# Who copies the first two key projections of a batch out of PSUM: ScalarE or VectorE

## The chip, the cores and the metric

One NeuronCore of a Trainium2 chip runs the whole program. The metric is the device time of one execution in microseconds (us).

## What is computed

The input has 32 batches of 256 tokens with 128 features. Each batch passes a layer norm, then an attention block with 16 heads of 64, and a feed-forward block beside it; both are added to the input.

```python
xn = _layernorm(x, axis=-1)
# attention on rmsnorm(xn) * norm_w:
q = x @ Wq;  k, v = jnp.split(x @ Wkv, 2, axis=-1)       # each 256 x 1024 per batch
q = _head_rmsnorm(q, q_gamma);  k = _head_rmsnorm(k, k_gamma)
sim = jnp.tanh(jnp.einsum('bhid,bhjd->bhij', q, k) / 50) * 50 * 64 ** -0.5
out = jnp.einsum('bhij,bhjd->bhid', jax.nn.softmax(sim), v)   # then @ Wo
# feed-forward: gelu(xn @ W1.T + low-rank part + b1) @ W2.T + low-rank part + b2
x = x + attention + feed_forward
```

## The kernel before

The engines run in a software pipeline over the batches. A period works on batch n in attention ("attn"), on n+1 in "front" (the second half of its projections, squares, norms, transposes of the heads), on n+2 in "turn" (its first projections), loads n+3 and finishes n-1. A period has eight steps, one for each pair of heads; the five lists TENSOR_STEPS, SCALAR_STEPS, VECTOR_STEPS, POOL_STEPS and the sync engine's loop say what each engine issues in each step, and in which order. The lists are in-order programs: an instruction that waits holds up everything behind it on its engine.

The names that matter here:

- **scores** (PE, L511) are the 12 matmuls of one pair into ps_scores; **tanh** (ACT, L597, tile clamped) reads them, **exp** (ACT, L604, tile probs) follows; **values** (PE, L537 to L539) multiplies probabilities with v two steps later into ps_o; **divide** (DVE, L772 and L776) takes ps_o out into o_sb.
- **q, k, v** with a number 0 to 3 are the projections of one batch: 128 tokens by 512 columns each, three matmuls L431, L432, L433 into one of three PSUM banks, ps_aux. Banks are used in turn, in the order of the tuples of three in TENSOR_STEPS, and `wait_bank` makes PE wait until the user three places back has been read.
- A **q** is squared by ACT (L623) and scaled by DVE (L799). A **v** is copied in bf16 by ACT (L633) and its remainder made by DVE (L804). A **k** is copied to qk by ACT (L628) and squared by POOL (L967); the sums of the squares are DVE's (L714).
- **normalise** (DVE, L755) writes a pair to ps_n, **half** (ACT, L612) makes its fp16 part and **halves** (DVE, L763) the remainder; two DMA transposes on the sync engine's queue (L396) then turn them for the scores three steps later.

By the order of the banks, k 0, k 1, v 2 stand in banks 0, 1, 2, and behind them v 3, q 2, q 3, and then k 2, k 3 and oT 0 of the next period. So in step 6 and the two steps behind it:

- v 3 waits until k 0 has been copied, q 2 until k 1 has;
- q 3 waits for DVE's part of v 2, k 2 for DVE's part of v 3;
- k 3 waits until q 2 has been scaled by DVE, oT 0 until q 3 has.

PE's step 6, for reference:

```python
    [("scores",), ("values",), ("k", 0, 2), ("k", 1, 2), ("y", 2), ("v", 2, 1), ("v", 3, 1)],
```

Of the kernel before, what the change touches and what calls it, by code (L numbers as in the profile page):

```python
# [32 lines left out]
PAIRS = HEADS // 2  # L33
# [43 lines left out]
    [("half", 3), ("tanh",), ("oT", 3, -1), ("exp",), ("half", 4), ("hid", 0, 0), ("hid", 1, 0)],  # L77
    [("tanh",), ("q", 0, 2), ("exp",)],
    [("half", 3), ("tanh",), ("q", 1, 2), ("exp",), ("v", 0, 1), ("v", 1, 1)],
    [("half", 3), ("tanh",), ("exp",), ("k", 0, 2), ("k", 1, 2), ("v", 2, 1)],  # L80
    [("half", 3), ("tanh",), ("v", 3, 1), ("exp",), ("q", 2, 2)],
]
VECTOR_STEPS = [
# [5 lines left out]
    [("divide",), ("newton", 5), ("newton", 6), ("newton", 7), ("newton", 8), ("normalise",), ("norm_stats",),  # L89
     ("q", 0, 2)],  # L90
    [("halves", 3), ("divide",), ("normalise",), ("q", 1, 2), ("sum", 0, 2), ("v", 0, 1)],
    [("halves", 3), ("v", 1, 1), ("divide",), ("normalise",), ("sum", 1, 2), ("v", 2, 1)],
    [("halves", 3), ("divide",), ("normalise",), ("v", 3, 1), ("sum", 2, 2), ("sum", 3, 2)],
]
POOL_STEPS = [
# [50 lines left out]
def block_kernel(nc, tokens, norm_w, wq, wkv, wo, q_gamma, k_gamma, w1, b1, w2, b2, scale, out):  # L146
# [6 lines left out]
    with ExitStack() as ctx:  # L153
# [50 lines left out]
        qk = sb("qk", [P, 2, TT, QK])  # L204
# [69 lines left out]
        qk_normed = sem("qk_normed")  # L274
# [7 lines left out]
        aux_filled = {k: sem(f"{k}_filled") for k in PER_BATCH}  # L282
        xT_split = sem("xT_split")
        xnT_copied = sem("xnT_copied")
        k_copied = sem("k_copied")
# [19 lines left out]
        def wait(eng, s, value):  # L305

            if isinstance(value, int) and value <= 0:
                return
            eng.wait_ge(s, value)
# [281 lines left out]
        @block.scalar  # L591
        def _(act):
            def tanh(st, pair):
                b, _, _ = st.batch(0)
                wait(act, scores_done, 2 * PAIRS * b + 2 * pair + 2)
                wait(act, probs_done, PAIRS * b + pair)
                nc.scalar.activation(clamped[:].rearrange("p j n -> p (j n)"),  # L597
                                     ps_scores[:].rearrange("p j n -> p (j n)"), ACT.Tanh).then_inc(clamp_done, 1)

            def exp(st, pair):  # L600
                b, _, _ = st.batch(0)
                wait(act, clamp_done, PAIRS * b + pair + 1)
                wait(act, attended, PAIRS * b + pair + 1 - RING)
                nc.scalar.activation(probs[:, pair % RING].rearrange("p j n -> p (j n)"),  # L604
                                     clamped[:].rearrange("p j n -> p (j n)"), ACT.Exp, bias=LIFT,
                                     scale=SOFTCLAMP * DH ** -0.5).then_inc(probs_done, 1)

            def half(st, ahead, pair):
                b, _, _ = st.batch(ahead)
                act.wait_ge(qk_normed, PAIRS * b + pair + 1)  # L610
                wait(act, heads_turned[pair % 4], 32 * ((PAIRS * b + pair) // 4))
                nc.scalar.copy(halves16[:, pair % 4, 0].rearrange("p a n -> p (a n)"), ps_n[:]).then_inc(half_hi_made, 1)  # L612

            def aux(st, kind, k, ahead):
                b, par, _ = st.batch(ahead)
                bank = bank_of(kind, k)
                act.wait_ge(aux_filled[kind], PER_BATCH[kind] * b + k + 1)
                if kind == "xT":
                    nc.scalar.copy(xhT_hi[:, par], bank[:, 0:seq])
                    nc.scalar.copy(xnT[:, b % 3], bank[:, seq:2 * seq]).then_inc(xnT_copied, 1)  # L620
                elif kind == "q":
                    wait(act, norm2_made, 8 * (b - 1) + 4 * (k // 2) + k % 2 + 1)
                    nc.scalar.activation(sq_q[:, k], bank, ACT.Square).then_inc(q_squared, 1)  # L623
                elif kind == "k":
                    if k == 0:
                        wait(act, qk_normed, PAIRS * (b - 1))
                    t, c = k // 2, 2 + k % 2
                    nc.scalar.copy(qk[:, par, t, c * 512:(c + 1) * 512], bank).then_inc(k_copied, 1)  # L628
                elif kind == "v":
                    if k == 0:  # L630
                        wait(act, attended, PAIRS * (b - 1))
                    t, c = k // 2, k % 2
                    nc.scalar.copy(v_hi[:, par, t, 8 * c:8 * c + 8, 0:DH],  # L633
                                   bank.rearrange("p (h d) -> p h d", d=DH)).then_inc(v_hi_made, 1)
                elif kind == "oT":
                    nc.scalar.copy(oT[:, 2 * k:2 * k + 2], bank.rearrange("p (j t) -> p j t", j=2))\
                        .then_inc(oT_copied, 1)
                elif kind == "hid":
                    for j in range(2):
                        c = 2 * k + j  # L640
                        nc.scalar.activation(hid[:, par, c], bank[:, j * seq:(j + 1) * seq], ACT.Gelu,  # L641
                                             bias=b1_col[:, c:c + 1]).then_inc(gelu_done, 1)

            def run(st):
                for s in range(PAIRS):
                    for what, *k in SCALAR_STEPS[s]:
                        if what == "tanh":
                            if "attn" in st.stages:
                                tanh(st, s)
                        elif what == "exp":  # L650
                            if "attn" in st.stages:
                                exp(st, s)
                        elif what == "half":
                            normed = ahead_of(st, s, *k)
                            if normed:
                                half(st, *normed)
                        elif STAGE[k[1]] in st.stages and (st.number > -2 or what != "xT"):
                            aux(st, what, *k)

            def weights_hi(c):  # L660
                part = slice(c * HEADS * DH, (c + 1) * HEADS * DH)
                act.wait_ge(w_scaled, c + 1)
                nc.scalar.copy(w_hi[:, part], w_raw[:, part]).then_inc(w_hi_made, 1)

            weights_hi(0)
            weights_hi(1)
            aux(Step(-1, 0, ()), *XT_TASK[1:])
            act.wait_ge(gammas_spread, 1)
            for j in range(2):
                nc.scalar.copy(g_bc[:, j * 512:(j + 1) * 512], ps_scores[:, j]).then_inc(gammas_copied, 1)  # L670
            weights_hi(2)
            act.wait_ge(ffn_turned, 1)
            nc.scalar.copy(b1_col[:], ps_o[:, 0:HC]).then_inc(ffn_copied, 1)
            nc.scalar.copy(w1T[:].rearrange("p a b -> p (a b)"), ps_scores[:, 0]).then_inc(ffn_copied, 1)
            nc.scalar.copy(w2T[:].rearrange("p a b -> p (a b)"), ps_scores[:, 1]).then_inc(ffn_copied, 1)
            act.wait_ge(ffn_copied, 3)
            run_all(act, run)
# [3 lines left out]
        def _(dve):  # L681
            v = nc.vector
# [106 lines left out]
            def aux(st, kind, k, ahead):  # L789
                b, par, _ = st.batch(ahead)  # L790
                bank = bank_of(kind, k)
                if kind == "xT":
                    xT_lo(st, bank)
                elif kind == "q":
                    dve.wait_ge(q_squared, 4 * b + k + 1)
                    if k == 0:
                        wait(dve, qk_normed, PAIRS * (b - 1))
                    t, c = k // 2, k % 2
                    v.tensor_tensor(qk[:, par, t, c * 512:(c + 1) * 512], bank, g_bc[:, c * 512:(c + 1) * 512],  # L799
                                    ALU.mult).then_inc(q_scaled, 1)  # L800
                elif kind == "v":
                    dve.wait_ge(v_hi_made, 4 * b + k + 1)
                    t, c = k // 2, k % 2
                    v.tensor_tensor(v_lo[:, par, t, 8 * c:8 * c + 8], bank.rearrange("p (h d) -> p h d", d=DH),  # L804
                                    v_hi[:, par, t, 8 * c:8 * c + 8, 0:DH], ALU.subtract).then_inc(v_split, 1)
                elif kind == "low":
                    dve.wait_ge(aux_filled["low"], 2 * b + k + 1)
                    if k == 1:
                        wait(dve, y_filled, b - 1)
                    o, base = (w1_eff[:], w1T) if k == 0 else (w2_eff[:, par], w2T)  # L810
                    v.scalar_tensor_tensor(o, bank.rearrange("p (c n) -> p c n", c=HC), scale_col[:, 0:1], base[:],
                                           ALU.mult, ALU.add)\
                        .then_inc(weff_made, 1)
# [220 lines left out]
```

## Time and profile before

| | |
|---|---|
| time, median of 3 runs | 1099.09 us (1098.5 to 1099.18) |
| the profiled execution | 1098.77 us, of which the span of the profile is 1096.6 us |
| PE (matmul) busy | 1048.1 us, 96% of the span |
| ACT busy | 1033.9 us, 94% |
| DVE busy | 928.6 us, 85% |
| POOL busy | 852.4 us, 78% |

PE is TensorE's matmuls, PEld its weight loads, ACT is ScalarE, DVE is VectorE, POOL is GpSimd, SPq the sync engine's DMA queue. A busy share says how full an engine is over the whole span; which engine sets the pace of a stage is read from the waits, the chain of work that ended last and the rows in order of time. In rows in order of time the first number is the start, the second the duration of the row (of all its instructions, for x2 and more), and square brackets give idle time just before it and who ended it. An instruction can start some 0.09 us before the end of the one ahead of it on its engine, because the ends overlap.

### The profile page before, as it was taken

The page shows a single profiled execution, that of the slowest core. Times are in us where ns is not written, and L with a number is a line of the kernel's source. Part 1 is how long each engine was busy: PE and PEld are TensorE (multiplying, and loading weights), DVE is VectorE, ACT ScalarE, POOL GpSimd, SP SyncE. Part 2 cuts the span into 40 slices and gives each one's busy share as a digit, 9 for nine tenths or more (in the row PEclk, how much of TensorE's full clock was granted, in tenths as well). Part 3 has the DMA queues.
Part 4 walks back from the last instruction along what each step waited for, and adds up shares of the span by engine and source line. Part 5 has one row for each costly group of instructions (what it writes and reads, how often), then busy time and mean ns, then how long its engine had stood idle before and what let it go on. Part 6 is the DMA issues. An engine that isn't in the chain of part 4 may idle for free.

```text
span 1096.6 us, 33887 instructions
## 1 busy us (share of the span) xinstructions
PE 1048.1 (96%) x12889; PEld 842.7 (77%) x12889; DVE 928.6 (85%) x2185; ACT 1033.9 (94%) x1545; POOL 852.4 (78%) x784
## 2 busy tenths in 40 slices
PE   5789999999999999999999999999999999999987
PEld 4467787777787777787777788777787777787776
DVE  6988889888889888889888889888889888889872
ACT  4699999999999999999999999999999999999996
POOL 7677878887878887878887878887878887878763
PEclk9899999999999999999999999999999999999999
DMA  3344444344454334444334444434444334344341
GB/s 114 65 72 81 74 85 80 71 78 84 74 84 80 74 77 82 75 85 79 75 75 84 75 84 80 72 77 84 76 83 79 78 71 84 76 82 80 65 92 31
DMA packets 310487, 85.41 MB, mean 78 GB/s; under 512 B 282020, under 2 KB 309816, under 8 KB 310328
## 3 DMA queue, kind: packets, MB, share of 16 engines
q1 hardware_dynamic: 310328, 83.25, 39.8%
q8 instruction: 104, 1.70, 0.7%
q14 instruction: 55, 0.45, 0.2%
HBM read 11.09 MB, written 4.19 MB: 14 GB/s over the span
## 4 chain that ended last, share of the span: by engine, by line
PE 42%; ACT 38%; issue 11%; SPq 2%; DVE 2%; POOL 2%; DMA 2%; ACTq 0%; POOLq 0%
ACT clamped L597 11%; PE ps_scores L511 10%; ACT probs L604 9%; PE ps_aux L486 5%; PE ps_aux L431 4%; PE ps_y L559 4%; ACT L641 4%; ACT halves L612 4%; ACT L604 4%; PE ps_o L537 3%; PE ps_aux L433 3%; PE ps_aux L432 3%; ACT hid L641 3%; PE ps_o L539 2%; PE ps_o L538 2%
## 5 line engine op out<-in xcount | busy, mean ns | idle before, releaser
L973 POOL TENSOR_TENSOR probs_lo<-probs 128x1024 f16<-128x1024 f32 x256 | 485.1, 1895 | 208.1 <-ACT probs L604 208.1
L597 ACT ACTIVATE clamped<-ps_scores 128x1024 f32<-128x1024 f32 x256 | 265.9, 1039 | 24.9 <-PE ps_scores L511 20.9
L604 ACT ACTIVATE probs<-clamped 128x1024 f32<-128x1024 f32 x256 | 273.0, 1066 | 2.6
L763 DVE TENSOR_TENSOR halves<-ps_n,halves 128x512 f16<-128x512 f32 x256 | 174.9, 683 | 65.9 <-ACT halves L612 65.8
L537 PEld LDWEIGHTS ps_o<-v_hi,probs 128*128 128x128 bf16 x2048 | 183.9, 98 | 60.9 <-issue 58.4
L511 PE MATMUL ps_scores<-heads_T 64*128 64x256 f16 x3072 | 212.2, 271 | 11.8 <-ACT clamped L597 6.1
L537 PE MATMUL ps_o<-v_hi,probs 128*128 128x65 bf16 x2048 | 213.8, 195 | 5.5 <-POOL probs_lo L973 1.4
L538 PE MATMUL ps_o<-v_lo,probs 128*128 128x64 bf16 x2048 | 211.7, 193 | 0.0
L539 PE MATMUL ps_o<-v_hi,probs_lo 128*128 128x65 bf16 x2048 | 211.3, 194 | 0.0
L431 PE MATMUL ps_aux<-w_hi,xhT_hi 128*128 128x512 f32 x384 | 178.9, 466 | 19.3 <-ACT qk L628 6.8
L538 PEld LDWEIGHTS ps_o<-v_lo,probs 128*128 128x128 bf16 x2048 | 187.3, 98 | 0.0
L539 PEld LDWEIGHTS ps_o<-v_hi,probs_lo 128*128 128x128 f16 x2048 | 187.2, 97 | 0.0
L511 PEld LDWEIGHTS ps_scores<-heads_T 64*128 64x128 f16 x3072 | 131.6, 94 | 65.6 <-issue 33.6
L755 DVE TENSOR_TENSOR ps_n<-qk,ps_o 128x512 f32<-128x512 f32 x256 | 175.8, 687 | 1.3
L612 ACT CAST halves<-ps_n 128x512 f16<-128x512 f32 x256 | 153.5, 599 | 3.8 <-DVE ps_n L755 3.4
L432 PE MATMUL ps_aux<-w_lo,xhT_hi 128*128 128x512 f32 x384 | 153.0, 398 | 0.0
L433 PE MATMUL ps_aux<-w_hi,xhT_lo 128*128 128x512 f32 x384 | 152.9, 398 | 0.0
L559 PEld LDWEIGHTS ps_y<-wo_sb,oT 128*128 128x128 f32 x1024 | 143.1, 191 | 10.5
L559 PE MATMUL ps_y<-wo_sb,oT 128*128 128x128 f32 x1024 | 150.3, 275 | 0.0
L967 POOL TENSOR_TENSOR sq_k<-qk 128x512 f32<-128x512 f32 x128 | 130.7, 1042 | 3.3 <-ACT qk L628 3.3
L431 PEld LDWEIGHTS ps_aux<-w_hi,xhT_hi 128*128 128x128 f32 x384 | 73.2, 191 | 69.8 <-DVE v_lo L804 25.3
L776 DVE TENSOR_TENSOR o_sb<-ps_o,rden 128x256 f32<-128x256 f32 x256 | 108.6, 424 | 8.8
(83 smaller groups left out, 1910.8 us busy)
## 6 DMA issues: line engine op xcount, KB each, us to landing
heads_T<-halves SPq DMA_TRANSPOSE x512, 2.5
x_in<-in_L_attn_tokens_dram SPq DMA_DIRECT2D x32, 128.0 KB, 2.4
x_res<-in_L_attn_tokens_dram SPq DMA_DIRECT2D x32, 128.0 KB, 2.3
out_dram<-y_sb SPq DMA_DIRECT2D x32, 128.0 KB, 2.0
sel_raw<-xn SPq DMA_DIRECT2D x192, 4.0 KB
qk<-in_L_attn_Wkv_dram SPq DMA_DIRECT2D x2, 512.0 KB, 5.6
qk<-in_L_attn_Wq_dram SPq DMA_DIRECT2D x1, 512.0 KB, 3.6
qk<-in_L_ffn_W_dram SPq DMA_DIRECT2D x2, 256.0 KB
```

Of the source, the lines that this page charges most:

```text
L431: pe.matmul(o, hi_l, hi_r, start=True, stop=False)
L432: pe.matmul(o, hi_l, lo_r, start=False, stop=False)
L433: return pe.matmul(o, lo_l, hi_r, start=False, stop=last)
L511: ins = pe.matmul(ps_scores[:, odd, t * seq:(t + 1) * seq], heads_T[rows, left, pair, t, k], heads_T[rows, right, pair, :, q], start=(i == ...
L537: pe.matmul(full, hi[:, col], v_hi[:, par, u, h], start=(u == 0), stop=False)
L538: pe.matmul(full[:, 0:DH], hi[:, col], v_lo[:, par, u, h], start=False, stop=False)
L539: ins = pe.matmul(full, probs_lo[:, buf, j, col], v_hi[:, par, u, h], start=False, stop=(u == TT - 1))
L559: ins = pe.matmul(o, oT[:, pair, tok], wo_sb[:, pair], start=False, stop=(i == n - 1))
L597: nc.scalar.activation(clamped[:].rearrange("p j n -> p (j n)"), ps_scores[:].rearrange("p j n -> p (j n)"), ACT.Tanh).then_inc(clamp_done, 1)
L604: nc.scalar.activation(probs[:, pair % RING].rearrange("p j n -> p (j n)"), clamped[:].rearrange("p j n -> p (j n)"), ACT.Exp, bias=LIFT, ...
L612: nc.scalar.copy(halves16[:, pair % 4, 0].rearrange("p a n -> p (a n)"), ps_n[:]).then_inc(half_hi_made, 1)
L973: g.tensor_tensor(probs_lo[:, buf].rearrange("p j n -> p (j n)"), probs[:, buf].rearrange("p j n -> p (j n)"), probs[:, buf].rearrange("p ...
```

## The change

ScalarE's step 6 loses the copies of k 0 and k 1. VectorE's step 6 gets them: k 0 between divide and normalise, k 1 between normalise and the sum of squares. The copies of k 2 and k 3, in step 0, stay with ScalarE. The semaphore k_copied is still counted in order, so each side waits for the other's earlier copies.

```diff
@@ SCALAR_STEPS, step 6
-    [("half", 3), ("tanh",), ("exp",), ("k", 0, 2), ("k", 1, 2), ("v", 2, 1)],
+    [("half", 3), ("tanh",), ("exp",), ("v", 2, 1)],
@@ VECTOR_STEPS, step 6
-    [("halves", 3), ("v", 1, 1), ("divide",), ("normalise",), ("sum", 1, 2), ("v", 2, 1)],
+    [("halves", 3), ("v", 1, 1), ("divide",), ("k", 0, 2), ("normalise",), ("k", 1, 2), ("sum", 1, 2), ("v", 2, 1)],
@@ scalar, aux
                 elif kind == "k":
-                    if k == 0:
-                        wait(act, qk_normed, PAIRS * (b - 1))
+                    wait(act, qk_normed, PAIRS * (b - 1))
+                    wait(act, k_copied, 4 * b + k)
@@ vector, aux
+                elif kind == "k":
+                    dve.wait_ge(aux_filled["k"], 4 * b + k + 1)
+                    if k == 0:
+                        wait(dve, qk_normed, PAIRS * (b - 1))
+                        wait(dve, k_copied, 4 * b)
+                    t, c = k // 2, 2 + k % 2
+                    v.tensor_copy(qk[:, par, t, c * 512:(c + 1) * 512], bank).then_inc(k_copied, 1)
```

VectorE's instructions in step 6 and the start of step 7 of a period, before. The rows begin with halves of step 6 and end with the scaling of q 2 and q 3 in step 0 of the next period (names in brackets are the semaphores waited for):

```order
L763 TENSOR_TENSOR halves16<-ps_n,halves16 128x512 [waits half_hi_made]
L804 TENSOR_TENSOR v_lo<-ps_aux,v_hi 128x512 [waits v_hi_made]
L772 RECIPROCAL rden<-ps_o 128x4 [waits attended]
L776 TENSOR_TENSOR o_sb<-ps_o,rden 128x2x128 [waits rden_made]
L755 TENSOR_TENSOR ps_n<-qk,ps_o 128x512 [waits half_lo_made]
L714 TENSOR_REDUCE norm2<-sq_q 128x8 [waits q_squared]
L804 TENSOR_TENSOR v_lo<-ps_aux,v_hi 128x512 [waits v_hi_made]
L763 TENSOR_TENSOR halves16<-ps_n,halves16 128x512 [waits half_hi_made]
L772 RECIPROCAL rden<-ps_o 128x4 [waits attended]
...
L799 TENSOR_TENSOR qk<-ps_aux,g_bc 128x512 [waits q_squared] x2
```

The same stretch on VectorE after the change (the two COPY rows are L807; what was L804 is now L811):

```order
L763 TENSOR_TENSOR halves16<-ps_n,halves16 128x512 [waits half_hi_made]
L811 TENSOR_TENSOR v_lo<-ps_aux,v_hi 128x512 [waits v_hi_made]
L772 RECIPROCAL rden<-ps_o 128x4 [waits attended]
L776 TENSOR_TENSOR o_sb<-ps_o,rden 128x2x128 [waits rden_made]
L807 COPY qk<-ps_aux 128x512 [waits k_copied,qk_normed,k_filled]
L755 TENSOR_TENSOR ps_n<-qk,ps_o 128x512 [waits half_lo_made]
L807 COPY qk<-ps_aux 128x512 [waits k_filled]
L714 TENSOR_REDUCE norm2<-sq_q 128x8 [waits q_squared]
L811 TENSOR_TENSOR v_lo<-ps_aux,v_hi 128x512 [waits v_hi_made]
L763 TENSOR_TENSOR halves16<-ps_n,halves16 128x512 [waits half_hi_made]
L772 RECIPROCAL rden<-ps_o 128x4 [waits attended]
...
L799 TENSOR_TENSOR qk<-ps_aux,g_bc 128x512 [waits q_squared] x2
```

Two copies stand ahead of everything from the sum of squares on, and one ahead of normalise; the order of the rest is the same.

ScalarE's step 6 before, from tanh to the half of step 7:

```order
L597 ACTIVATE clamped<-ps_scores 128x1024 [waits probs_done,scores_done]
L604 ACTIVATE probs<-clamped 128x1024 [waits attended,clamp_done]
L628 COPY qk<-ps_aux 128x512 [waits qk_normed,k_filled]
L628 COPY qk<-ps_aux 128x512 [waits k_filled]
L633 CAST v_hi<-ps_aux 128x8x64 [waits v_filled]
L612 CAST halves16<-ps_n 128x512 [waits heads_turned2,qk_normed]
```

And after:

```order
L597 ACTIVATE clamped<-ps_scores 128x1024 [waits probs_done,scores_done]
L604 ACTIVATE probs<-clamped 128x1024 [waits attended,clamp_done]
L633 CAST v_hi<-ps_aux 128x8x64 [waits v_filled]
L612 CAST halves16<-ps_n 128x512 [waits heads_turned2,qk_normed]
```

The bf16 copy of v 2 and the half of step 7 stand right behind exp. PE's, POOL's and the sync engine's programs are the same as before.

## Rows read from the trace of the kernel before

**Rows 1.** Busy time in nine stretches of 100 us: their sum and mean.

```profile
sum 900.00, PE 884.79 PEld 713.51 DVE 784.97 ACT 875.84 POOL 720.65; mean PE 98.31 PEld 79.28 DVE 87.22 ACT 97.32 POOL 80.07
```

**Rows 2.** Waits, whole span: total us, times, longest us.

```profile
PEld ps_aux L431 <- ACT qk L628: 20.3, 31, 1.1
...
PE ps_aux L431 <- ACT qk L628: 6.8, 31, 0.7
```

**Rows 3.** The chain that ended last, 500 to 570 us: start, us, what.

```profile
528.60 0.58 ACT qk L628
...
529.22 0.50 PE ps_aux L431
...
545.54 0.82 ACT clamped L597
```

**Rows 4.** ACT in order of time, steps 6 and 7 of one period.

```profile
528.60 1.06 ACT L628 COPY qk<-ps_aux 128x512 f32<-128x512 f32 x2
529.54 0.60 ACT L633 CAST v_hi<-ps_aux 128x512 bf16<-128x512 f32 x1
530.02 0.61 ACT L612 CAST halves<-ps_n 128x512 f16<-128x512 f32 x1
531.02 1.03 ACT L597 ACTIVATE clamped<-ps_scores 128x1024 f32<-128x1024 f32 x1 [0.39 <-PE ps_scores L511]
```

**Rows 5.** PE in order of time: v 2's last, v 3's first, k 3's first matmul.

```profile
528.62 0.40 PE L433 MATMUL ps_aux<-w_hi,xhT_lo 128*128 128x512 f32 x1
529.22 0.50 PE L431 MATMUL ps_aux<-w_hi,xhT_hi 128*128 128x512 f32 x1 [0.20 <-ACT qk L628]
...
536.13 0.46 PE L431 MATMUL ps_aux<-w_hi,xhT_hi 128*128 128x512 f32 x1
```

**Rows 6.** DVE in order of time, from halves of step 6 to q 2.

```profile
526.71 0.69 DVE L763 TENSOR_TENSOR halves<-ps_n,halves 128x512 f16<-128x512 f32 x1 [0.19 <-ACT halves L612]
...
528.12 0.42 DVE L776 TENSOR_TENSOR o_sb<-ps_o,rden 128x256 f32<-128x256 f32 x1
528.46 0.69 DVE L755 TENSOR_TENSOR ps_n<-qk,ps_o 128x512 f32<-128x512 f32 x1
529.05 0.68 DVE L714 TENSOR_REDUCE norm<-sq_q 128x8 f32<-128x512 f32 x1
530.18 0.69 DVE L804 TENSOR_TENSOR v_lo<-ps_aux,v_hi 128x512 bf16<-128x512 f32 x1 [0.45 <-ACT v_hi L633]
530.78 0.68 DVE L763 TENSOR_TENSOR halves<-ps_n,halves 128x512 f16<-128x512 f32 x1
531.82 0.18 DVE L772 RECIPROCAL rden<-ps_o 128x4 f32<-128x4 f32 x1 [0.35 <-PE ps_o L539]
...
535.36 1.27 DVE L799 TENSOR_TENSOR qk<-ps_aux,g_bc 128x512 f32<-128x512 f32 x2
```

**Rows 7.** PE's weight loads in order of time: the first of k 3.

```profile
536.09 0.19 PEld L431 LDWEIGHTS ps_aux<-w_hi,xhT_hi 128*128 128x128 f32 x1 [0.23 <-DVE qk L799]
```
**Rows 8.** DVE by form, whole span: busy us, mean ns of one, idle before.

```profile
L799 DVE TENSOR_TENSOR qk<-ps_aux,g_bc 128x512 f32<-128x512 f32 x128 | 83.9, 676 | 2.5 <-ACT sq_q L623 2.3 <-issue 0.2
...
L811 DVE SCALAR_TENSOR_TENSOR w_eff<-ps_aux,scale_col,w1T 128x512 f32<-128x512 f32 x32 | 23.7, 742 | 0.0
...
L737 DVE TENSOR_TENSOR ps_o<-newton_r,ps_o 128x64 f32<-128x64 f32 x96 | 21.7, 226 | 2.2
...
L727 DVE TENSOR_SCALAR newton_r<-ps_o 128x64 int32<-128x64 int32 x32 | 7.2, 224 | 1.1
```

**Rows 9.** DVE in order of time, before the first period.

```profile
13.13 0.78 DVE L818 TENSOR_SCALAR qk<-qk,nw_col 128x1024 f32<-128x1024 f32 x1
...
21.62 0.69 DVE L714 TENSOR_REDUCE norm<-sq_k 128x8 f32<-128x512 f32 x1 [0.91 <-POOL sq_k L967]
...
38.24 0.69 DVE L804 TENSOR_TENSOR v_lo<-ps_aux,v_hi 128x512 bf16<-128x512 f32 x1 [0.48 <-ACT v_hi L633]
```

**Rows 10.** Sync engine's queue in order of time, step 0 of the next period.

```profile
538.55 2.52 SPq L396 DMA_TRANSPOSE heads_T<-halves  x2
```

## The prediction

> **What bounds the kernel now.** I began with the busy time by stretches. Between 100 and 1000 us the mean is PE 98.3, ACT 97.3, DVE 87.2 of 100 us [rows 1]. Two engines are full and the third has room, so the change looks like relief for a full one. Shares can't say which of the two holds the end in which step, so I read the chain of work next. Two hand-overs repeat in it in every period [rows 3]. At 529.22 the chain goes from ACT's copy of k 0 (528.60 + 0.58 = 529.18) to PE's first matmul of v 3; from there PE holds it through steps 7, 0, 1 and 2 until tanh of step 3 at 545.54, and from there ACT holds it to step 6 again. So **ACT sets the pace from step 3 to the middle of step 6, PE from there to step 3**. The waits over the whole span say the same: a matmul of the L431 kind waits for ACT's k copy 31 times, once per period, 20.3 us by the weight loads and 6.8 us by the matmuls [rows 2].
>
> Then I read one period in order of time. PE ends v 2 and sits idle 0.20 us until k 0 is out of its bank [rows 5]. Matmuls of that kind follow each other with a spacing of some 0.24 us, so v 3 could have begun at 528.62 + 0.24 = 528.86, and the wait is worth 0.36 us at most. ACT, behind its two copies, gets to v 2 and half, and then waits 0.39 us for PE's scores of step 7 [rows 4]: time given back to ACT here is waited away.
>
> **The change on ScalarE.** Two copies go, 1.06 us together, some 0.94 us of queue (528.60 to 529.54, [rows 4]). What is gained there is not 30 x 0.94: tanh of step 7 is held by PE. The only thing that PE waits for is k 0's bank. v 2's bf16 copy now comes as soon as PE has filled the bank: 528.62 + 0.40 = 529.02, so it ends at about 529.65 instead of 530.14.
>
> **The change on VectorE.** What does one copy cost there? No row shows a single-source 512-column DVE instruction out of PSUM. The nearest are the 512-column ones with one PSUM operand: 676 ns for the scaling of q, 742 ns for the scalar_tensor_tensor [rows 8]. In the queue they cost less, since ends overlap: normalise at 528.46, the next at 529.05, 0.595 us apart [rows 6]. From below: a single-source instruction from SBUF to SBUF took 0.78 us for 1024 columns [rows 9], twice as fast per column, which for 512 would be some 0.78 - 0.27 = 0.51 us long, 0.42 in the queue. Does that rate hold out of PSUM? The 64-column rows say no: a column costs (676 - 226) / 448 = 1.0 ns in tensor_tensor, so double rate would make a single-source 64-column instruction some 32 ns shorter than a tensor_tensor; the one that reads PSUM (L727) takes 224 ns against 226 [rows 8]. I take 0.595 us in the queue and 0.68 us from start to end; the bounds are 0.42 and 0.66 (742 ns less the same overlap).
>
> The Trainium skill (VectorE: DVE Perf Modes, Why PSUM operands drop a tier) says that a PSUM operand caps fp32 at the single rate. The 224 ns row agrees. Its cycle table gives 120 + 512 cycles, an estimate of 658 ns for the copy; with it each number below would be about 0.02 us smaller. At the double rate the sum would have the other sign, which is the second rival.
>
> **k 0's hand-over.** DVE starts k 0 where normalise started, at 528.46; its bank was full long before. It ends at 529.14 against 529.18 on ACT. PE gains 0.04 us of the 0.36. The reason is that DVE comes to k 0 only behind halves, v 1 and divide, and halves had waited for ACT's half (idle 0.19 before 526.71, [rows 6]); ACT was the pace-setter up to there, so that start doesn't move.
>
> **DVE's debt.** Two copies push everything behind them by 2 x 0.595 = 1.19 us. Two gaps take some of it. Between the sum at 529.05 and v 2's remainder at 530.18 there is 1.13 us where 0.595 is needed: 0.53 spare (it was the wait for ACT's v 2, which now comes early enough). Between halves at 530.78 and the reciprocal at 531.82, 1.04 where 0.60 is needed: 0.44 spare; this was the wait for PE's values, and they end no later than before. Together 0.97. The debt left is 1.19 - 0.97 = **0.22 us**. From 531.82 to 535.36 no row shows idle time, so it is carried whole to the scaling of q 2: start 535.57 instead of 535.36, end 536.25 instead of 535.36 + 0.68 = 536.04.
>
> **Who waits for it.** PE's k 3 uses q 2's bank. Before, its weights were loaded at 536.09, just 0.05 us behind the end of q 2's scaling, after 0.23 us of waiting [rows 7], and its matmul came at 536.13, with no time lost to speak of [rows 5]. DVE was exactly on time, with nothing to spare. Now the load comes at 536.30 and the matmul at 536.30 to 536.34: PE is late by 0.17 to 0.21 us, in the stretch that PE sets. Behind k 3, q 3's scaling holds oT 0 by the same amount, nothing more is lost there, and PE carries the delay to tanh of step 3 and so into the period. The 0.04 us gained at v 3 drowns in the wait for q 2.
>
> The other waiters have slack. k 1 is out at about 530.3 and q 2 is multiplied behind the values at 531.6. Remainders of v 2 and v 3 end 0.65 and 0.2 us later, still ahead of q 3 and k 2. Halves of step 7 is 0.65 us later (531.43); its transposes are for scores three steps on, and the sync queue is itself behind: the next pair's transposes are issued at 538.55 [rows 10], three us after their halves. Normalise of step 6 is 0.6 us later, at 529.05 to 529.74; half of step 7 started at 530.02. POOL's squares start behind probs_lo.
>
> **Sum.** Batches whose k 0 and k 1 are projected beside attention: 30 of 32 (two are in the fill). 30 x 0.2 = 6.0 us. In the fill DVE is the longest: for the first batch the copies stand behind the weight split instead of beside it, and 0.9 us of idle before the sums [rows 9] takes most of it, about 0.25 left; for the second the debt is 1.19 less the 0.48 + 0.09 before v 2's remainder, 0.6, of which I count 0.5. Total 6.0 + 0.75 = 6.75 us on the profiled execution's 1098.77: 1105.5. The median of the runs is 0.3 us above that execution, so **1105.8 us**, 0.6% slower. With the bounds of the copy's cost: at 0.66 the debt is 0.35, 10.5 us and 1 in the fill, 1110.6; a debt of zero needs 0.485.
>
> **Rivals.**
> - *The debt is lost in slack.* If rests of a few hundredths between DVE's instructions or an earlier start of its chain take most of the 0.22, only the fill is left: 1099.09 + 0.75 = 1099.8, no change. For it: 0.22 is a small difference of large numbers. Against: no idle shown from 531.82 to 535.36. Chance 0.12.
> - *The copy is fast* (faster than before). A single-source DVE copy out of PSUM at double rate: 0.42 in the queue. Debt 0.84, all absorbed by 0.97; k 0 is out at 528.46 + 0.51 = 528.97, PE starts v 3 at 529.01, 0.21 earlier; 30 x 0.21 = 6.3, 1092.8 us. It decides below 0.485 us in the queue. For it the 0.78 row, against it the 224 ns row. Chance 0.06.
> - *ScalarE is what counts.* If its 0.94 us came off each period: 30 x 0.94 = 28, 1071 us. Against: its 0.39 us wait in step 7 and the PE-held chain. 0.02.
> - *More than the debt gets through:* the 0.65 us lateness of halves in step 7 reaches the scores through the sync queue, 30 x 0.65 = 19.5, 1119 us. Against: three steps between. 0.05.
>
> **How the numbers follow.** The forecast has 0.75. Its own spread (debt 0.1 to 0.35, fill 0.3 to 1.2) is 1102.4 to 1110.6; the range 1101.5 to 1110 holds it and the edge of the first rival. Within 0.2% (2.2 us) is about what a measurement of this kernel can tell from no change: faster 0.08, same 0.13, slower 0.79.
>
> **What the changed profile would show.** DVE's k copies at about 0.68 us each; k 0 ending 0.04 us sooner in the period than ACT's did; the reciprocal of step 7 no longer waiting for PE; PE's L431 matmuls waiting for DVE's scaling of q, some 0.2 us, 30 times, in step 0; ACT idle about 0.5 to 1 us more in steps 6 and 7 of each period; one batch to the next about 0.2 us longer. I am wrong if the copy takes clearly less than 0.6 us, if DVE shows idle time between step 6's halves and q 2's scaling, or if PE waits at another place.

## The result and the profile after

| | before | changed |
|---|---|---|
| median | 1098.8 us (4 runs, 1098.25 to 1099.18) | 1105.86 us (4 runs, 1105.18 to 1106.12) |
| ratio | | 1.0064, 95% interval 1.0046 to 1.0081 |
| profiled execution, its span | 1098.77, 1096.6 us | 1105.18, 1103.1 us |

The changed kernel is slower by 7 us, 0.64%, at the same granted clock (0.995 in both profiles). Its page begins so (busy time and instructions of each engine, then the chain of work that ended last, by engine):

```profile
PE 1056.0 (96%) x12889; PEld 844.7 (77%) x12889; DVE 961.5 (87%) x2249; ACT 1012.1 (92%) x1481; POOL 851.6 (77%) x784
...
PE 34%; ACT 34%; DVE 22%; issue 9%; DMA 0%; ACTq 0%; SPq 0%; POOL 0%
```

ACT has lost 22 us of work, DVE has gained 33 us. The chain tells more than the shares: DVE is only 87% busy, but it holds 22% of the chain now, where it held 2% before:

```profile
PE 42%; ACT 38%; issue 11%; SPq 2%; DVE 2%; POOL 2%; DMA 2%; ACTq 0%; POOLq 0%
```

The mean by stretches, beside [rows 1], shows the same with PE as full as ever:

```profile
sum 900.00, PE 885.30 PEld 709.66 DVE 808.20 ACT 853.14 POOL 717.78; mean PE 98.37 PEld 78.85 DVE 89.80 ACT 94.79 POOL 79.75
```

The chain in order of time (start, us, what) has three hand-overs per period now, where [rows 3] had two. ACT gives to DVE at halves of step 6, DVE holds it for 9.6 us, and PE gets it at k 3, which waits for the scaling of q 2:

```profile
529.88 0.64 ACT halves L612
530.54 0.69 DVE halves L763
...
539.48 0.61 DVE qk L799
540.13 0.50 PE ps_aux L431
...
549.58 0.81 ACT clamped L597
```

DVE in that stretch, to be laid beside [rows 6]:

```profile
530.54 0.69 DVE L763 TENSOR_TENSOR halves<-ps_n,halves 128x512 f16<-128x512 f32 x1 [0.18 <-ACT halves L612]
...
531.95 0.42 DVE L776 TENSOR_TENSOR o_sb<-ps_o,rden 128x256 f32<-128x256 f32 x1
532.29 0.68 DVE L807 COPY qk<-ps_aux 128x512 f32<-128x512 f32 x1
532.89 0.69 DVE L755 TENSOR_TENSOR ps_n<-qk,ps_o 128x512 f32<-128x512 f32 x1
533.48 0.68 DVE L807 COPY qk<-ps_aux 128x512 f32<-128x512 f32 x1
534.09 0.67 DVE L714 TENSOR_REDUCE norm<-sq_q 128x8 f32<-128x512 f32 x1
534.68 0.68 DVE L811 TENSOR_TENSOR v_lo<-ps_aux,v_hi 128x512 bf16<-128x512 f32 x1
535.28 0.68 DVE L763 TENSOR_TENSOR halves<-ps_n,halves 128x512 f16<-128x512 f32 x1
535.88 0.17 DVE L772 RECIPROCAL rden<-ps_o 128x4 f32<-128x4 f32 x1
...
539.40 1.28 DVE L799 TENSOR_TENSOR qk<-ps_aux,g_bc 128x512 f32<-128x512 f32 x2
```

Both gaps of [rows 6] are gone, in front of v 2's remainder and in front of the reciprocal. Measured from the start of halves in step 6, q 2 is scaled at 539.40 - 530.54 = 8.86 us, before at 535.36 - 526.71 = 8.65. PE, matmuls and then the weight load of k 3, beside [rows 5, 7]:

```profile
533.03 0.50 PE L431 MATMUL ps_aux<-w_hi,xhT_hi 128*128 128x512 f32 x1 [0.18 <-DVE qk L807]
...
540.13 0.50 PE L431 MATMUL ps_aux<-w_hi,xhT_hi 128*128 128x512 f32 x1
```
```profile
540.13 0.19 PEld L431 LDWEIGHTS ps_aux<-w_hi,xhT_hi 128*128 128x128 f32 x1 [0.49 <-DVE qk L799]
```

v 3 starts 2.49 us behind halves (before 2.51), k 3 9.59 us (before 9.42): 0.02 us gained, 0.17 lost. k 3's own first matmul costs 0.04 more as well: the next one follows after 0.34 us, before after 0.30. Its weights are loaded only as it starts (both rows at 540.13), before 0.04 us ahead. The matmul's row shows no idle time, since the end of the matmul ahead of it is modelled; the weight load's row shows the wait. Medians over 25 periods say the same: k 3's first matmul is 0.19 us later behind halves than before, its second 0.22, and PE's instructions stay 0.21 to 0.22 later to the end of the period. So the whole loss of a period arises at k 3.

ACT, beside [rows 4], has waits of 0.35 and 0.63 us where there was one of 0.39, and tanh of step 7 starts 4.28 us behind halves, before 4.31. The 0.94 us of queue that the two copies left free is waited away:

```profile
532.88 0.59 ACT L633 CAST v_hi<-ps_aux 128x512 bf16<-128x512 f32 x1 [0.35 <-PE ps_aux L433]
533.61 0.58 ACT L612 CAST halves<-ps_n 128x512 f16<-128x512 f32 x1
534.82 1.03 ACT L597 ACTIVATE clamped<-ps_scores 128x1024 f32<-128x1024 f32 x1 [0.63 <-PE ps_scores L511]
```

The whole span's waits (total us, times, longest): behind the scaling of q the weight loads waited 16.2 us before and 24.2 now. The 20.3 us behind ACT's k copy [rows 2] are now 20.0 us behind DVE's, so that wait has changed its releaser and not its size:

```profile
PEld ps_aux L431 <- DVE qk L799: 24.2, 35, 3.6
PEld ps_aux L431 <- DVE qk L807: 20.0, 31, 1.5
```

A copy took what the prediction took for it (by form: busy us, mean ns):

```profile
L807 DVE COPY qk<-ps_aux 128x512 f32<-128x512 f32 x64 | 43.6, 682 | 0.5 <-PE ps_aux L433 0.5
```

**The account of the two spans.** I date a period by the start of v 0's remainder on DVE. From one batch to the next it is 32.86 us before and 33.07 us after. In the profile of before three of 29 periods were longer, by 0.34, 0.23 and 0.41 us; after, none. The first period with all stages begins at 65.47 us before and at 66.73 us after; behind the last start both need the same 45.45 us. So the spans differ by 1.26 (fill) + 30 x 0.205 (6.15) - 0.98 (the three long periods of before) = 6.4 us, against 1103.1 - 1096.6 = 6.5.

The 1.26 us of the fill are the net of two things. Ahead of PE's only long wait for a transpose in the fill, PE is 1.73 us late (L492 at 50.82, before at 49.09). Then the transposes come, and PE waits 0.84 us for them, before 1.94:

```profile
52.05 0.86 PE L511 MATMUL ps_scores<-heads_T 64*128 64x256 f16 x12 [0.84 <-DMA heads_T<-halves]
```
```profile
51.41 0.83 PE L511 MATMUL ps_scores<-heads_T 64*128 64x256 f16 x12 [1.94 <-DMA heads_T<-halves]
```

### The profile page after: what moved, and what is told of

The parts are those of the page before. It is cut to its first block, busy times and chain, and to the rows that moved or that the text cites. A ratio compares the mean times of both kernels' runs of the same rounds, so it can differ in the third digit from the quotient of the medians.

```text
span 1103.1 us, 33952 instructions
## 1 busy us (share of the span) xinstructions
PE 1056.0 (96%) x12889; PEld 844.7 (77%) x12889; DVE 961.5 (87%) x2249; ACT 1012.1 (92%) x1481; POOL 851.6 (77%) x784
## 4 chain that ended last, share of the span: by engine, by line
PE 34%; ACT 34%; DVE 22%; issue 9%; DMA 0%; ACTq 0%; SPq 0%; POOL 0%
ACT probs L604 9%; ACT clamped L597 8%; PE ps_scores L511 8%; PE ps_aux L486 5%; DVE halves L763 5%; DVE v_lo L811 4%; DVE norm L714 4%; ACT L641 4%; ACT halves L612 4%; ACT L604 4%; PE ps_y L559 3%; DVE qk L807 3%; PE ps_aux L431 3%; ACT hid L641 3%; DVE ps_n L755 3%
## 5 line engine op out<-in xcount | busy, mean ns | idle before, releaser
L763 DVE TENSOR_TENSOR halves<-ps_n,halves 128x512 f16<-128x512 f32 x256 | 174.9, 683 | 65.5 <-ACT halves L612 65.4
```

The costliest lines, as they stand in the source:

```text
L763: v.tensor_tensor(halves16[:, pair % 4, 1].rearrange("p a n -> p (a n)"), ps_n[:], halves16[:, pair % 4, 0].rearrange("p a n -> p (a n)"), ...
```

## The experiments

The period is read from each kernel's trace in the same way (one execution each); ratios are to the kernel before on the same chip (medians 1098.64, 1099.56 and 1098.69 us for the three groups of four). "Few waits" means: without the added waits on ScalarE that the order doesn't need.

| kernel | median us | ratio, 95% interval | period us |
|---|---|---|---|
| two blanks on VectorE | 1103.85 | 1.0049, 1.0036 to 1.0063 | 33.05 |
| three blanks | 1122.06 | 1.0213, 1.0199 to 1.0227 | 33.65 |
| k 0 alone on VectorE | 1100.29 | 1.0014, 1.0005 to 1.0023 | 32.88 |
| k 1 alone on VectorE | 1101.96 | 1.0024, 1.0013 to 1.0035 | 32.91 |
| changed, q 2 scaled first | 1101.51 | 1.0021, 1.0013 to 1.0030 | 32.93 |
| changed, k 0 ahead of divide | 1105.59 | 1.0062, 1.0050 to 1.0075 | 33.06 |
| k 0 on VectorE ahead of divide, k 1 on ScalarE | 1088.12 | 0.9898, 0.9886 to 0.9911 | 32.47 |
| before, k 0 ahead of exp | 1085.87 | 0.9880, 0.9865 to 0.9894 | 32.39 |
| k 0 alone, few waits | 1098.12 | 0.9993, 0.9984 to 1.0002 | 32.83 |
| k 0 ahead of divide, few waits | 1087.22 | 0.9894, 0.9882 to 0.9907 | 32.47 |
| changed, few waits | 1104.75 | 1.0058, 1.0046 to 1.0070 | 33.07 |
| fill only | 1099.42 | 1.0004, 0.9995 to 1.0012 | 32.85 |

**Two and three blank instructions.** The debt on VectorE without any move of a copy, against the kernel before (the lines that allocate blank and its semaphore are left out; three blanks have a `("blank", 2)` behind the second, and 3 in place of 2 in the wait):

```diff
-    [("halves", 3), ("v", 1, 1), ("divide",), ("normalise",), ("sum", 1, 2), ("v", 2, 1)],
+    [("halves", 3), ("v", 1, 1), ("divide",), ("blank", 0), ("normalise",), ("blank", 1), ("sum", 1, 2), ("v", 2, 1)],
+                        elif what == "blank":
+                            if "attn" in st.stages and "turn" in st.stages:
+                                wait(dve, blank_made, 2 * st.batch(0)[0])
+                                v.tensor_reduce(blank[:, k[0]], g_bc[:, 0:512].rearrange("p (h d) -> p h d", d=DH),
+                                                AX_X, ALU.add).then_inc(blank_made, 1)
```

> The kernel before, with two more VectorE instructions per period and nothing else: a 512-column reduce that nobody reads stands where the changed kernel has its copies of k 0 and k 1 (behind divide, behind normalise of step 6). ScalarE keeps both copies. Theory (VectorE's debt: 2 x 0.595 less 0.97 of gaps is 0.22 us, which reaches PE at k 3): the loss of the change without its relief and without its cost in the fill, 30 x 0.2 = 6 us, less up to 1 us for three periods that were irregular before: 1104 to 1105 us, k 3's matmul of step 0 about 0.2 us late behind q 2's scaling. Rival (the loss comes from who copies k: a hand-over of semaphores between two engines, PSUM read by VectorE): no change, 1099.

> The same with a third reduce behind the second. The gaps are used up by the second, so the third should be paid whole: debt 3 x 0.595 - 0.97 = 0.81 us, 30 x 0.8 = 24, 1122 us. If the waits merely get longer where there is slack elsewhere, less than 1115.

Two blanks give a period of 33.05 us, 0.02 from the changed kernel's, though ScalarE does all its old work. The third adds 0.60 us per period, a whole instruction's share of the queue. The waits of weight loads and matmuls behind the scaling of q, with two blanks:

```profile
PEld ps_aux L433 <- DVE qk L801: 22.2, 35, 2.1
...
PE ps_aux L433 <- DVE qk L801: 6.3, 6, 1.4
```

and with three:

```profile
PEld ps_aux L433 <- DVE qk L801: 40.1, 35, 2.1
...
PE ps_aux L433 <- DVE qk L801: 24.2, 35, 1.4
```

With two, the wait shows on the weight loads and hardly on the matmuls; with three the matmuls wait too, in every period, at the named place. Who copies k, and across which semaphore, has at most 0.02 us in the period's loss of 0.21. The median with two blanks, 1103.85, is just under my 1104, that with three as expected.

**One copy alone.** k 0 (`("k", 1, 2)` back on ScalarE behind exp) and k 1 (`("k", 0, 2)` back). The edit for k 0, step 6 of ScalarE and then of VectorE, against the kernel before; the waits of the change stay, and VectorE's copy waits for the count `4 * b + k` of k_copied (not shown):

```diff
-    [("half", 3), ("tanh",), ("exp",), ("k", 0, 2), ("k", 1, 2), ("v", 2, 1)],
+    [("half", 3), ("tanh",), ("exp",), ("k", 1, 2), ("v", 2, 1)],
-    [("halves", 3), ("v", 1, 1), ("divide",), ("normalise",), ("sum", 1, 2), ("v", 2, 1)],
+    [("halves", 3), ("v", 1, 1), ("divide",), ("k", 0, 2), ("normalise",), ("sum", 1, 2), ("v", 2, 1)],
```

> Only k 0 moves to VectorE (same place, behind divide); k 1 stays with ScalarE behind exp. Theory: one copy is 0.595 us, less than the 0.97 of gaps, so no debt; PE gets k 0's bank 0.04 us earlier, 31 x 0.04 = 1.2 us gained, some of it given back in the fill: 1097.5 to 1099.5. Rival (a copy ahead of normalise delays halves and scores, and this is what costs): about half of the loss of the change or more, 1102 to 1105.

> Only k 1 moves to VectorE (behind normalise); k 0 stays with ScalarE behind exp. Theory: no debt, and k 0's hand-over is where it was: 1098.5 to 1099.5. Rival as for k 0 alone, now with the copy behind normalise: if the loss is due to the copy in front of normalise, this one is free and the other isn't; by the debt both are free.

In the period both are nearly free (0.02 and 0.05 us), and the one behind normalise is no cheaper than the one in front of it. k 3's first matmul comes 9.38 and 9.41 us behind halves (medians), before 9.41: no debt reaches it. But both medians missed my ranges on the slow side, and that of k 1, 1101.96, comes near the rival's 1102; only the periods tell the two apart. I had a gain of 0.04 per period for k 0 and nothing for k 1. Laid period on period from halves of step 6, k 0's kernel is 0.02 us ahead of the one before, and k 1's level with it, up to PE's second oT in step 1; from there they are 0.04 and 0.06 us behind. ACT shows why (k 0's kernel: k 1, which waited for the count of DVE's k 0; then k 2 and k 3 of step 0):

```profile
530.78 0.59 ACT L628 COPY qk<-ps_aux 128x512 f32<-128x512 f32 x1 [0.56 <-DVE qk L807]
...
538.36 1.26 ACT L628 COPY qk<-ps_aux 128x512 f32<-128x512 f32 x2
```

From the start of k 2 to the end of k 3 it takes 1.26 us, 1.06 before; the change put two more semaphore waits in front of each. The copies themselves are no longer (0.56 and 0.58 us; before 0.57 and 0.59). k 3 starts later: here k 2 runs from 538.36 to 538.92 and k 3 starts at 539.03; before, k 3 started at 537.32, ahead of the end of k 2 at 537.42.

```profile
539.03 0.58 ACT L628 COPY qk<-ps_aux 128x512 f32<-128x512 f32 x1
```
```profile
537.32 0.59 ACT L628 COPY qk<-ps_aux 128x512 f32<-128x512 f32 x1
```

The count `4 * b + 3` of k_copied for which k 3 waits is the one that k 2's copy gives, so ScalarE waits for its own last instruction and loses the overlap with it (k 3's other added wait, for qk_normed, was not tried apart). k 2 starts 0.97 us behind exp with or without the added waits. tanh of step 1 and the oT behind it slip by what is left.

The profiled execution of k 1's kernel was 4.2 us longer than that of the kernel before; it was the longest of its seven. Its first full period begins 3.8 us later and its periods are 30 x 0.05 us longer, against the 0.98 us of the three long periods before. In the fill PE waited 2.73 us once for a transpose of the heads, at a place where it waited 1.94 before; why that transpose was later there stays open.

**Few waits.** Only those that the order of the two engines needs, in three of the kernels, against the change (where both copies are on VectorE, the condition is k == 2 and the wait is the one for k_copied alone):

```diff
-                    wait(act, qk_normed, PAIRS * (b - 1))
-                    wait(act, k_copied, 4 * b + k)
+                    if k == 1:
+                        wait(act, qk_normed, PAIRS * (b - 1))
+                        wait(act, k_copied, 4 * b + k)
```

> k 0 alone on VectorE, as before, but ScalarE's copies of k 2 and k 3 in step 0 no longer carry the two extra semaphore waits each that the change gave them. In the trace of k 0 alone those two copies took 1.26 us instead of 1.06, tanh of step 1 came 0.14 us later, and from PE's second oT on (step 1) everything was 0.06 us later, which would be the difference between the 0.02 us gained at v 3 and the 0.025 us lost per period. Theory: the waits cost it, so a period of 32.83 to 32.85 us instead of 32.88, 1098 to 1099.3 with the fill. Rival (something else, ScalarE's wait for k_copied in front of k 1 say): 32.88 as before, 1100.3.

> The changed kernel with as few waits in front of ScalarE's k 2 and k 3 as the order of the two engines allows (one). There PE is 0.2 us late at k 3, so that ScalarE's 0.14 us in step 1 should be hidden: 33.06 us per period and 1105 to 1106.5 as before. If the waits were part of the loss: 33.01 or less, 1104.

> k 0 on VectorE ahead of divide, k 1 on ScalarE, without the extra waits in front of k 2 and k 3. Theory: 0.05 us per period less than the 32.47 with them, near the 32.39 of ScalarE's k 0 ahead of exp: 1086 to 1087. Rival: 32.47, 1088.

With k 0 alone, k 2 and k 3 are back at 1.05 us, and the time came out as expected:

```profile
536.32 1.05 ACT L629 COPY qk<-ps_aux 128x512 f32<-128x512 f32 x2
```

and the period at 32.83, 0.03 below before. The changed kernel keeps its 33.07: there PE is late anyway. Its k 2 still waits for k_copied, its k 3 no longer, and the two are back at 1.06 us, so it is the wait in front of k 3 that cost. Its median, 1104.75, is 1 us lower and a little under my range, within the scatter of the two. The third was a miss: 32.47 stayed, so in that kernel something else sets the period (next but one).

**Where the debt reaches PE.** The changed kernel with q 2 scaled one place earlier (VectorE's step 0), and with k 0 copied one place earlier (its step 6), each against the change:

```diff
-    [("halves", 3), ("q", 2, 1), ("q", 3, 1), ("divide",), ("normalise",), ("result",), ("sum", 4, 1)],
+    [("q", 2, 1), ("halves", 3), ("q", 3, 1), ("divide",), ("normalise",), ("result",), ("sum", 4, 1)],
```
```diff
-    [("halves", 3), ("v", 1, 1), ("divide",), ("k", 0, 2), ("normalise",), ("k", 1, 2), ("sum", 1, 2), ("v", 2, 1)],
+    [("halves", 3), ("v", 1, 1), ("k", 0, 2), ("divide",), ("normalise",), ("k", 1, 2), ("sum", 1, 2), ("v", 2, 1)],
```

> The changed kernel, with one exchange on VectorE in step 0: q 2 is scaled ahead of halves instead of behind it, so 0.60 us earlier. Theory (PE pays at k 3, which waits for q 2): k 3 is on time again, q 3 (for oT 0) is still 0.2 us late but its matmuls need it 0.7 us after k 3, so at most 0.05 us per period is left: the fill's 1.3 us and 0 to 1.5 us, 1099 to 1101.5. Rival (the debt reaches PE by normalise or halves and the scores): no better than the changed kernel, 1106, or worse since halves is later still.

> The changed kernel with k 0 copied ahead of divide instead of behind it. PE gets the bank 0.55 us earlier, so v 3 starts about 0.3 us earlier than in the kernel before. Theory: VectorE's chain from step 6 to q 2 has the same length, so this is wasted at k 3: 1105.5 to 1106.5, with PE's wait at q 2 about 0.3 us longer. Rival (k 0's late hand-over is what costs): 0.3 x 31 = 9 us gained, 1097.

The exchange of two neighbours in step 0 takes the period from 33.07 to 32.93, two thirds of the loss, with not an instruction less on DVE. PE's medians behind halves show where the 0.07 left arise. k 3's second matmul is now 0.09 us earlier than in the kernel before; oT 0, which waits for q 3 (first row below), is 0.02 later, and the scores behind it 0.07. From PE's second oT in step 1 on, where the added wait on ACT showed in the lone copies, at most 0.02 more is lost. So nearly all of it is q 3; I had expected 0.05 at most.

Freeing k 0's bank one place earlier, 0.55 us, on the other hand, brings nothing: PE starts v 3 0.34 us sooner than in the changed kernel and waits the longer for q 2, with k 3 at 9.60 us behind halves in both (last two rows; 24.2 and 7.0 us in the changed kernel):

```profile
PEld ps_aux L486 <- DVE qk L799: 11.7, 30, 0.7
```
```profile
PEld ps_aux L431 <- DVE qk L799: 38.3, 35, 3.7
...
PE ps_aux L431 <- DVE qk L799: 22.9, 35, 3.2
```

**The same early bank, without the debt.** k 0 on VectorE ahead of divide, k 1 on ScalarE (step 6 of ScalarE, then of VectorE, against the kernel before; the waits as for k 0 alone):

```diff
-    [("half", 3), ("tanh",), ("exp",), ("k", 0, 2), ("k", 1, 2), ("v", 2, 1)],
+    [("half", 3), ("tanh",), ("exp",), ("k", 1, 2), ("v", 2, 1)],
-    [("halves", 3), ("v", 1, 1), ("divide",), ("normalise",), ("sum", 1, 2), ("v", 2, 1)],
+    [("halves", 3), ("v", 1, 1), ("k", 0, 2), ("divide",), ("normalise",), ("sum", 1, 2), ("v", 2, 1)],
```

And with ScalarE alone, the kernel before with one copy moved:

```diff
-    [("half", 3), ("tanh",), ("exp",), ("k", 0, 2), ("k", 1, 2), ("v", 2, 1)],
+    [("half", 3), ("tanh",), ("k", 0, 2), ("exp",), ("k", 1, 2), ("v", 2, 1)],
```

> k 0 on VectorE ahead of divide, k 1 on ScalarE behind exp. Theory: one copy makes no debt, and PE's wait for k 0's bank (0.36 us at most) is gone, with the steps behind it 0.3 us earlier: 31 x 0.3 = 9 us, 1089 to 1091. It is less if the sync queue's transposes, which made PE wait in three periods of the kernel before, can't follow: then 1093 to 1097.

> The kernel before, with ScalarE's copy of k 0 between tanh and exp of step 6 instead of behind exp; nothing on VectorE. Theory: k 0's bank is free at 528.2 instead of 529.18, v 3 doesn't wait, 31 x 0.35 = 11 us at best; exp of step 6 is 0.5 us later, for which POOL has some room: 1088 to 1091. The same bound by the transposes as in the run before: 1093 to 1097.

Both beat both kernels, 1.0% and 1.2% faster than before, and both are faster than I had expected (1089 and 1088 at best). The first, in the version with few waits, shows why waits no longer matter to it. DVE runs without a gap again:

```profile
523.35 0.68 DVE L808 COPY qk<-ps_aux 128x512 f32<-128x512 f32 x1
...
526.28 0.68 DVE L764 TENSOR_TENSOR halves<-ps_n,halves 128x512 f16<-128x512 f32 x1
526.88 0.17 DVE L773 RECIPROCAL rden<-ps_o 128x4 f32<-128x4 f32 x1
```

The reciprocal follows halves at once, for PE's values are earlier too. One copy (0.6) in 0.97 of gaps leaves 0.38, and 0.39 is what the period lost. PE agrees: its instructions behind v 3 come 0.48 us earlier behind halves than before, up to k 3; there the weight load waits for q 2 (row below), and 0.38 is left. So DVE sets this kernel's period, and a further gain would have to come off DVE.

```profile
531.14 0.19 PEld L431 LDWEIGHTS ps_aux<-w_hi,xhT_hi 128*128 128x128 f32 x1 [0.34 <-DVE qk L800]
```

In ScalarE's version the copy stands where exp waits for tanh anyway:

```profile
518.90 1.08 ACT L597 ACTIVATE clamped<-ps_scores 128x1024 f32<-128x1024 f32 x1
519.82 0.64 ACT L628 COPY qk<-ps_aux 128x512 f32<-128x512 f32 x1
520.28 1.14 ACT L604 ACTIVATE probs<-clamped 128x1024 f32<-128x1024 f32 x1
```

exp comes 1.38 us behind the start of tanh, against some 1.11 without the copy, so that the copy costs ScalarE 0.27 us of queue there instead of 0.47. PE shows what the period gained (v 2's last, then v 3's first two matmuls, beside [rows 5]):

```profile
521.00 0.39 PE L433 MATMUL ps_aux<-w_hi,xhT_lo 128*128 128x512 f32 x1
521.23 0.40 PE L431 MATMUL ps_aux<-w_hi,xhT_hi 128*128 128x512 f32 x1
521.47 0.39 PE L432 MATMUL ps_aux<-w_lo,xhT_hi 128*128 128x512 f32 x1
```

v 3 starts 0.23 us behind v 2's last matmul, before 0.60; and its second matmul follows 0.24 us behind its first, before 0.34, when the weights were loaded only as the first one started. From v 3's second matmul on PE is 0.47 us earlier behind halves (medians), to the end of the period, and 32.86 - 32.39 is 0.47. PE's wait for the bank is thus worth 0.36 us in its own right and 0.11 in the matmul behind it. In this profile PE also waited for late transposes in the middle of the span, three times, 0.34, 1.23 and 0.57 us.

**The fill.** VectorE copies k 0 and k 1 of the first two batches only (the lists as in the change, with `("k", 0, 2)` and `("k", 1, 2)` back in ScalarE's step 6; ScalarE's wait for k_copied only for the first two batches, not shown):

```diff
+                        if what == "k" and "attn" in st.stages:                  # vector
+                            continue
+                        if what == "k" and s == 6 and "attn" not in st.stages:   # scalar
+                            continue
```

> VectorE copies k 0 and k 1 only for the two batches of the fill; from the first period with attention on it is the kernel before. The trace of the changed kernel has the first full period 1.26 us later than before, where the prediction counted 0.75. Theory: the fill's part is fixed and nothing of it is regained later: 1098.7 + 1.3 = 1100, periods of 32.86. If slack in the first periods absorbed it: 1099.

1099.42 against 1098.69 us, an interval from 0.5 us below to 1.3 us above before: a fill cost of 0.75 and one of 1.26 both fit, and so does none. The traces speak for a cost: the first period with all stages begins between 64.2 and 65.5 us in the four kernels without VectorE copies in the fill and between 65.7 and 69.3 us in the ten with them. Each is one execution, and the starts differ among the ten by more than the cost, so its size stays open.

## Why the prediction was right, point by point

- **What bounds the kernel.** ACT sets the pace up to step 6 and PE from there: borne out by the two kernels that take away the wait at the hand-over and gain 1%. The blanks show that a third engine counts as soon as its gaps are used.
- **A copy costs 0.595 us of queue and 0.68 us.** Measured 0.60 (532.29 to 532.89) and 682 ns, so the copy did not run at the double rate. The Trainium skill (VectorE: DVE Perf Modes, Why PSUM operands drop a tier) says the same of fp32 with a PSUM operand. The estimate of 658 ns, by the cycle table of the Trainium skill (VectorE: DVE Perf Modes, The TRN2 errata), is 24 ns low.
- **k 0's hand-over gains 0.04 us.** Measured 0.02. That the whole wait is worth 0.36 us at most was too little: freed in time it gave 0.47, because v 3's first matmul got shorter by 0.11. This had no part in the forecast.
- **Gaps of 0.97 us, a debt of 0.22.** Measured 0.21 (8.86 against 8.65). The lone copies and the third blank bear it out from both sides: one instruction brings no delay to k 3, the third is paid whole.
- **k 3 pays, by 0.17 to 0.21 us.** Measured 0.17 plus 0.04 in its first matmul, 0.205 per period. The exchange of q 2 and halves shows the place; the early bank for k 0 shows that nothing ahead of it counts. That k 3 lost no time to speak of before is off by a little: with q 2 scaled earlier its second matmul came 0.09 us sooner than in the kernel before.
- **The fill, 0.75 us.** The profile after has 1.26, and 1.73 ahead of the wait for the transposes. By that profile this term was too small; the timed fill-only kernel can't tell.
- **A term that I had not:** before, three periods in which PE waited for late transposes were 0.98 us longer together; after, none was. Whether the longer period hides such waits isn't shown (the kernels at 32.47 had none either). This happens to cancel the shortfall in the fill.
- **The total is luck to the decimal.** 1105.5 was forecast for the profiled execution, which took 1105.18; the median was to lie 0.3 us above it and lay 0.68 above. So 1105.8 and 1105.86 are closer than their parts. The stated spread also ran to 1110.6, past the range's 1110.
- **A statement that missed something.** I counted two copies off ScalarE and nothing added to it. The added wait in front of k 3 cost it 0.2 us per period in step 0. In the changed kernel this is covered by PE's delay, which is why the sum didn't suffer; with k 0 alone, where that delay is missing, it was worth 0.05 us per period (32.88 against 32.83).

## What to carry to other kernels

Moving work to the engine with idle time is paid for by the idle time in one stretch, not by its share over the span: add up the gaps between the point where that engine's timing is fixed and the first place where someone waits for it, and compare with what is added. Here 13% idle was 0.97 us where two copies needed 1.19, and one copy would have fit. If an engine waits for a bank, moving the instruction that frees it up by one place in its own queue can be worth more than moving it to another engine (here 1.2% faster instead of 0.6% slower). And a semaphore that two engines count in order can make an engine wait for its own last instruction: leave out the waits that its own order already gives.

## What the runs showed of the hardware

- A ScalarE copy of 128x512 started 0.47 us behind the start of the one ahead of it, 0.10 before that one's end. When it had to wait for the count which that one gives, it started 0.11 behind its end, 0.67 behind its start, and the pair took 1.26 us instead of 1.06. Where ScalarE isn't waited for this is free; with k 0 alone it was some 30 x 0.05 = 1.5 us over the span.
- A projection's first matmul whose weights could be loaded 0.23 us ahead was followed by the next after 0.24 us; when its weights were loaded only as it started, behind a wait for the bank, after 0.34.
- A ScalarE copy put between tanh and the exp that waits for tanh's result cost 0.27 us of the queue, not the 0.47 of a copy between others.
- Transposes by DMA were late now and then: in the kernel before, three periods of 29 were 0.2 to 0.4 us longer, with rows like this one on PE:

```profile
314.63 0.83 PE L511 MATMUL ps_scores<-heads_T 64*128 64x256 f16 x12 [0.27 <-DMA heads_T<-halves]
```
